# A decoder layer on one core: where the rotary products of q and k are made

## What is computed

```python
x = x + attention(layernorm(x))            # 16 heads of 32, rotary, causal
x = x + ssm(ctx, gate=layernorm(x))        # 16 states for each of 512 channels, gated
x = x + ffn(layernorm(x))                  # ternary weights, absmax scaling, exact gelu
```

```python
q, k, v = layernorm(x) @ w_qkv
rotary(x) = concat(x1 * cos - x2 * sin, x2 * cos + x1 * sin)
scores = rotary(q) @ rotary(k).T / sqrt(32)      # causal, softmax, @ v, @ w_o
```

## Time and profile before

| | |
|---|---|
| median of 3 runs | 1167.27 us (1163.96 to 1167.78) |
| the profiled execution | 1165.5 us |
| its span | 1163.7 us |
| busy in the span | TensorE 987.3 us, VectorE 956.9, ScalarE 808.1, GpSimd 623.8 |
| granted TensorE clock, mean | 0.921 |

### The profile page before, as it was taken

How to read it: one execution, slowest core, us unless ns; L and a number is a source line. 1 busy time by engine, 2 the same in 40 slices (tenths; PEclk the granted TensorE clock), 3 DMA queues, 4 the chain that set the end, 5 groups by cost and what they waited for, 6 DMA issues and landing times.

```text
span 1163.7 us, 18250 instructions
## 1 busy us (share of the span) xinstructions
PE 987.3 (85%) x5652; PEld 737.4 (63%) x5652; DVE 956.9 (82%) x1351; ACT 808.1 (69%) x1539; POOL 623.8 (54%) x509
## 2 busy tenths in 40 slices
PE   6857988789988999788999877586698889889997
PEld 3335765557755677655568656464577777778875
DVE  6458699884689976897997899899999999999654
ACT  5534787765488666798776998746988878884432
POOL 1257367764336667546665762476655555554411
PEclk8878989899989999889999986688898999899999
DMA  6215552444325653333464361430111110000000
GB/s 204 95 37 168 186 163 84 132 129 155 106 84 167 198 164 109 101 106 121 129 197 157 95 220 50 154 119 14 49 49 36 32 34 22 33 19 10 19 19 19
DMA packets 59358, 115.87 MB, mean 100 GB/s; under 512 B 8880, under 2 KB 13232, under 8 KB 58240
## 3 DMA queue, kind: packets, MB, share of 16 engines
q1 hardware_dynamic: 59264, 114.70, 31.4%
HBM read 90.42 MB, written 24.25 MB: 99 GB/s over the span
## 4 chain that ended last, share of the span: by engine, by line
PE 48%; DVE 21%; issue 11%; POOL 9%; ACT 8%; DMA 1%; SPq 1%; DVEq 0%; POOLq 0%; ACTq 0%
PE ps L1642 9%; PE ps L1710 6%; DVE hb L1804 5%; PE ps L1723 5%; PE ps L1784 5%; PE ps L1656 4%; PE ps L1682 4%; DVE y_acc L1826 4%; POOL hb L1253 3%; PE ps L1695 3%; PE ps L1774 3%; PE ps L1764 2%; DVE m_col L1900 2%; DVE fh L2030 2%; PE ps L1668 2%
## 5 line engine op out<-in xcount | busy, mean ns | idle before, releaser
L1253 POOL TENSOR_TENSOR hb<-du,b_bc 128x1024 f32<-128x1024 f32 (+1 forms) x160 | 313.4, 1978 | 175.0 <-PE ps L1710 174.2
L1804 DVE TENSOR_TENSOR_SCAN hb<-ps,hb 128x1024 f32<-128x1024 f32 (+1 forms) x128 | 257.7, 2015 | 31.2 <-ACT ps L1382 21.8
L1382 ACT ACTIVATE ps<-delta,a_neg 128x511 f32<-128x511 f32 (+2 forms) x320 | 180.0, 598 | 76.3 <-DVE hb L1804 69.1
L1710 PE MATMUL ps<-ident,hb 128*128 128x128 f32 x1088 | 169.6, 299 | 49.1 <-DVE hb L1804 20.3
L1826 DVE SCALAR_TENSOR_TENSOR y_acc<-ps,ct,y_acc 128x512 f32<-128x512 f32 x256 | 182.6, 742 | 29.2 <-PE ps L1710 28.2
L1710 PEld LDWEIGHTS ps<-ident,hb 128*128 128x128 f32 x1088 | 135.2, 153 | 80.2 <-issue 42.2
L1493 ACT ACTIVATE p_q<-ps,m_col 128x512 f32<-128x512 f32 (+3 forms) x256 | 131.4, 526 | 27.7 <-DVE m_col L1900 24.9
L1642 PE MATMUL ps<-xn_t,w_ring 128*128 128x512 f32 x256 | 124.4, 632 | 3.7 <-DVE tmp L1881 1.8
L1682 PE MATMUL ps<-ident,p_q 128*128 128x128 f32 x640 | 97.6, 298 | 22.7 <-ACT p_q L1493 17.9
L1509 ACT ACTIVATE p_t<-ps 128x512 f32<-128x512 f32 x160 | 87.8, 597 | 40.2 <-PE ps L1682 39.6
L1774 PE MATMUL ps<-t_fc,xq_hi 128*128 128x512 f32 x256 | 106.4, 416 | 10.0 <-DVE xq_lo L2015 6.5
(11 more groups left out here) (147 smaller groups left out, 1953.2 us busy)
## 6 DMA issues: line engine op xcount, KB each, us to landing
w_ring<-in_w_attn SPq DMA_DIRECT2D x32, 512.0 KB, 3.8
qk_d<-hl SPq DMA_DIRECT2D x64, 256.0 KB
q_st<-qk_d SPq DMA_DIRECT2D x128, 128.0 KB, 2.7
b_bc<-bc_d SPq DMA_DIRECT2D x48, 256.0 KB, 3.5
k_st<-qk_d SPq DMA_DIRECT2D x64, 128.0 KB, 2.7
k_st<-qk_d SPq DMA_DIRECT2D x128, 64.0 KB, 2.3
x_in<-in_x SPq DMA_DIRECT2D x16, 256.0 KB, 3.1
raw_fc<-in_w_fc SPq DMA_DIRECT2D x4, 1024.0 KB, 7.9
```

What stands on the lines that cost most here:

```text
L1253: nc.gpsimd.tensor_tensor(piece_of(e, hi, lo).rearrange("p (a n) -> p a n", a=2), du[b % 2][:, 2 * h:2 * h + 2, lo:hi], b_bc[:, i % BC_RIN ...
L1382: ins = nc.scalar.activation(factors(j, hi, lo)[:, (hi - lo) * m + start:(hi - lo) * (m + 1)], delta[b % 2][:, et, lo + start:hi], ACT.Exp ...
L1710: mm = nc.tensor.transpose(bank(kind, *a)[:, P * et:P * et + P], piece_of(2 * r + et // 2, hi, lo)[:, at:at + P], ident[:])
L1804: v.tensor_tensor_scan(h, d, h, 0.0, ALU.mult, ALU.add).then_inc(scan_done, 1)
```

## The change

In batches two to four (b > 0) a ScalarE item `rot` takes each half out of PSUM with one copy, to `tmp[:, 2]` and `tmp[:, 3]`. When the second half has been copied, GpSimd multiplies both by cosine into `tmp[:, 0:2]`, then by sine in place, and goes on with the subtraction and the addition as before. Batch one stays with VectorE. The plan is told 0.6 us for each ScalarE copy and 7 us for GpSimd's step instead of 2.6, and the VectorE shares of 1.4 us are gone. The count of freed banks now asks `emptied_by(item)` for the engine.

```diff
@@ WEIGHT @@
- 'act': {'carry': -3.3,
+ 'act': {'rot': 0,
+         'carry': -3.3,
...
+def rot_by(b):
+    return "act" if b > 0 else "dve"
+
+def emptied_by(item):
+    return rot_by(item[1]) if item[0] == "rot" else EMPTIED_BY.get(item[0])
@@ follows @@
         yield "pe", 3.5, [act("ln1b", b, LT - 1), sp("wload", CHUNK_OF[kind, b, n])]
-        yield "dve", 1.4, [pe(*item)] + ([dve("rot", b, n, 0)] if half else [])
+        who = rot_by(b)
+        yield who, 1.4 if who == "dve" else 0.6, [pe(*item)] + ([(who, ("rot", b, n, 0))] if half else [])
         if half:
-            yield "pool", 2.6, [dve(*item)]
+            yield "pool", 2.6 if who == "dve" else 7, [(who, item)]
@@ plan @@
-        reader = READER.get(kind) or (kind == "ht" and y_reader(item))
+        reader = emptied_by(item) or READER.get(kind) or (kind == "ht" and y_reader(item))
...
-    for _n, _item in enumerate(x for x in ORDER[_who] if EMPTIED_BY.get(x[0]) == _who):
+    for _n, _item in enumerate(x for x in ORDER[_who] if emptied_by(x) == _who):
@@ gpsimd, kind == "rot" @@
                     emptied(pool, TASK[(kind, *a)])
+                    if rot_by(b) == "act":
+                        halves = tmp[:, 2:4, :]
+                        consts(pool, "rotary")
+                        nc.gpsimd.tensor_tensor(tmp[:, 0:2, :], halves, cos[:].unsqueeze(1).to_broadcast([P, 2, L]), ALU.mult)
+                        own.done(nc.gpsimd.tensor_tensor(halves, halves, sin[:].unsqueeze(1).to_broadcast([P, 2, L]), ALU.mult))
+                        own.settle()
                     nc.gpsimd.tensor_tensor(tmp[:, 0, :], tmp[:, 0, :], tmp[:, 3, :], ALU.subtract)
@@ scalar @@
+                elif kind == "rot":
+                    b, n, half = a
+                    if half == 0:
+                        scratch_free(act, (kind, b, n))
+                    act.wait_ge(m_full, TASK[(kind, *a)] + 1)
+                    nc.scalar.activation(tmp[:, 2 + half, :], bank(kind, *a), ACT.Copy).then_inc(m_free["act"], 1)
```

## The result

| | before | after |
|---|---|---|
| median of 4 runs | 1165.62 us (1162.73 to 1167.78) | 1196.64 us (1193.46 to 1199.44) |
| span of the profiled execution | 1163.7 us | 1194.6 us |
| granted TensorE clock, mean | 0.921 | 0.912 |

The change costs 31.0 us, a ratio of 1.0249 [1.0219, 1.0279]. The direction was forecast; the time lies above the range, and the forecast's +8 us is about a quarter of what came. Beside the first, third, fourth and fifth experiment two of before's thirteen executions were slow (2378 and 2986 us); they are in no ratio, and without them before's median there is 1165.74 us and not 1166.18.

What follows compares the result with a forecast made beforehand. Rotary stretches were taken as bound by TensorE and VectorE in turn. Against 1165.5 us: -8.0 (products off the chain) + 6.6 (copies) + 9.5 (GpSimd, half) = +8.1, said as 1174 us; range 1157 to 1188, the forecast case's own 1170 to 1188.

Steps and rivals of the forecast that it cites:

- the pieces of VectorE's products on the chain: Rotary stretches: 19 pieces of VectorE's PSUM products, at 11 of 24 halves, come off the last-ending chain, -8.0 us.
- What is late next: Scratch tile between rotary pairs: held 4.0 us longer a pair, 16 us a batch; later loads costed at nothing.
- the lower end is nothing, for the order is worked out anew: GpSimd's longer rotary step: replanning can put ScalarE's hi copy behind other work, so the added cost could be nothing.
- half of 19.0 us taken for GpSimd: GpSimd's longer rotary step: middle of 0 and 19.0 taken as its cost, 9.5 us.
- a gain or loss of several us: Stretches without rotary pairs: the order worked out anew may gain or lose several us there.
- if the order stays: GpSimd's longer step at four of twelve pairs on the chain: 4 x 4.74 = 19.0 us, the upper end.
- 17.6 with the exchange: Rotary stretches: exchanging VectorE products for ScalarE copies, -1.4 us, with GpSimd's full 19.0 gives +17.6.
- VectorE's relief: Rival, rotary stretches: GpSimd's addition is absorbed and freed VectorE decides, 1150 to 1163 us; chance 0.30.
- the two cancel: Rival, rotary step: hidden on both sides, time within 0.3%, 1164 to 1171 us; chance 0.17.
- The scratch tile's chain: Rival, queues behind each batch's pairs: late by 16 us, 16 to 48 us lost, 1181 to 1213 us; chance 0.08.
- a sign of the forecast: Rotary stretches: more waits of VectorE's scans for GpSimd's product would show the forecast right.
- the Trainium skill's warning: VectorE and GpSimd share a port, so moving work might not help; by it alone +16 us.

Runs made afterwards that it cites:

- the first: Kernel before, only the plan told 7 us instead of 2.6 for GpSimd's rotary step in batches two to four: 1191.78 us, +25.6, 1.0202.
- third: Kernel before plus four extra GpSimd products of 128x512 behind each lo of batches two to four, outside the scratch tile, planned: 1191.82 us, +25.6, 1.0212.
- fourth: Kernel before, scratch tile in batches two to four passed on only when the pair's store has landed, plan told: 1207.08 us, +40.9, 1.0331.
- fifth experiment: Changed kernel, ScalarE's copies of the next pair wait only for GpSimd's rotary step, not for lo, plan told: 1166.64 us, +0.5, 1.0005.
- five new orders: Before's instructions replanned: GpSimd's step told as 2.9 us (+12.1) or 7 us (+25.6), or planner constant PATIENCE 0.28 (+26.4), 0.32 (+35.1), 0.34 (+13.2) instead of 0.3.
- the kept order: Changed kernel planned with before's engine and times, only the 24 halves moved from VectorE's list to ScalarE's at their planned times: 1209.30 us, +41.1, 1.0351.
- in four: After's instructions planned with planner constant PATIENCE 0.28 (+31.4), 0.3 (+31.0, the change itself), 0.32 (+29.2) and 0.34 (+27.3), against before.
- the early release: Next pair's ScalarE copies wait only for GpSimd's rotary step, not lo: after replanned +0.5 (PATIENCE 0.3), +0.4 (0.32); after in before's order 1210.25 us, +42.0.
- ten orders with the late release: Before's instructions in five new orders and after's in five, scratch tile freed at lo: 12 to 51 us above before.
- the four with 0.32 and 0.34: Planner constant PATIENCE 0.32 and 0.34 instead of 0.3: before's instructions +35.1 and +13.2, after's +29.2 and +27.3, against before.
- The early release with 0.32: Changed kernel with copies waiting only for GpSimd's rotary step, planner constant PATIENCE 0.32 instead of 0.3: 1168.51 us, +0.4, 1.0001 against before.
- before's order at 0.3: The unchanged kernel before, planned with planner constant PATIENCE at its original 0.3: 1165.62 us.
- before with early release: Kernel before, scratch rows exchanged between pairs so the next pair's first half waits only for GpSimd's step, plan told: 1165.64 us, -0.9, 0.9987.

## Why the forecast was right in sign and too small

**Right: the operations.** All four GpSimd durations and the copies were right, and the busy totals of GpSimd and ScalarE within 3 us. The step's four products are gone from VectorE's rows (32.8 us), but its busy time fell by 20.4 and not 33. A part of the gap of 12.4 is an overlap of the records that I did not allow for. Before, timeline of VectorE, two products of one half, 0.61 us apart though each lasts 0.69:

```profile
562.68 0.69 DVE L1880 TENSOR_TENSOR tmp<-ps,cos 128x512 f32<-128x512 f32 x1 [0.78 <-PE ps L1642]
563.29 0.68 DVE L1881 TENSOR_TENSOR tmp<-ps,sin 128x512 f32<-128x512 f32 x1
```

At 0.08 us for each of 48 that is at most 3.8 us. The last section has another 5.6; some 3 us stay open. Much of this is the order's: before's own instructions have a busy VectorE of 957.1 to 966.1 us in their five new orders, and in the kept order the change's fell by 27.3 (956.9 to 929.6). One reading of the rows was off without effect: the pieces of VectorE's products on the chain are 21, not 19; their 8.0 us and the 11 halves are right.

**Failed step: "What is late next", put into the sum at nothing.** The prediction had seen that the tile is held 4.0 us longer a pair, 16 us a batch, and that eight of nine passages are tight; it gave the hold no term of its own, costed the late loads behind the pairs at nothing "while TensorE has scan transposes to run", and left the rest to a rival with 0.08. It is what the loss goes with: the pairs of a batch spread by 6.7, 7.5 and 8.9 us, the fourth `lo` is late by 12, 19 and 31, and with the tile released early the same instructions are at +0.5 and +0.4. The way was another than told there. The projection does not start when the tile is free, but where the plan has put it, which is at the planned release; no engine of after waits for the tile.

**Failed step: "the lower end is nothing, for the order is worked out anew", and half of 19.0 us taken for GpSimd.** The new order was counted as free cover. It does cover: `hi` waits 14.3 us in after and 48.5 in the kept order, and the time is 10 us less. But it has a price of its own, which the sum lacked. Before's own instructions lose 12 to 35 us in five new orders (+12.1, +13.2, +25.6, +26.4, +35.1, mean 22.5), and after's, in four, 27 to 31 (mean 29.7). A fifth order of after's instructions, with 2.6 us told, lost 51.2; it is left out of that mean because its told time is far from the real one, though the 7 us told to before's (+25.6) is in the other. The last paragraph of the prediction allowed for "a gain or loss of several us" from this; on before's own instructions it is larger than any term of the sum, and I gave it no line there. What is left for the change itself is 29.7 - 22.5 = 7 us, or 4.4 by the paired values, near the forecast's 8.1 (up to the first `fc`: 25.7 - 18.5 = 7.2). With before's orders spread over 23 us, no run shows that this agreement is more than luck; with the fifth order counted it would be 34.0 - 22.5 = 11.5.

**Failed step: the upper end "if the order stays", 19.0 us (17.6 with the exchange).** It measured 41.1. I charged the 4.74 us to the four pairs at which before's chain runs through GpSimd. But that chain shows who was last then, and a longer step is last elsewhere too. GpSimd's result comes 4.0 us later at each of twelve pairs (4.74 less the 0.77 of the shorter ScalarE copy), and `hi` waits 43.8 / 12 = 3.65 us longer: by that the queues held some 0.3 us in hand on average. 12 x 4.0 = 48 us, less that, would have been the bound to write down. That these waits are what makes the 41.1 is argued and not shown; the 25.1 us at the copies stand beside them.

**The rivals.** VectorE's relief did not decide, nor did the two cancel. The scratch tile's chain, given 0.08 and 1181 to 1213 us, is the one that fits: 1196.6 lies in its range, and a shorter hold told to the plan, with the long step kept, takes all of the loss back in two orders. It is not shown that the hold does this by itself. With the order kept, the early release changed nothing (+42.0 for +41.1), and no run has the order of the early release with the late wait. Nor does all that an unfitted order loses come from this tile: ten orders with the late release lie 12 to 51 us above before, but the four with 0.32 and 0.34 lose 9 to 10 us of it behind the last pair. The early release with 0.32 loses 7.6 there too, behind 4.8 us gained ahead of the first `fc`. What I had against this rival, TensorE idle for a tenth only, was no argument: TensorE does other work while the pairs slip, and pays behind them, with 11.5 us more of idle time between the last pair and the first `fc`, which starts at 828 us and not at 796.

**Also not as forecast.** The scans did not wait more for GpSimd's product (4.3 us between 187 and 640 us before, 4.2 after). They did with the early release, 19.3 us, in the kernel that loses nothing: the wait named as a sign of the forecast is no sign of the loss. In after they waited for ScalarE's exponentials, and VectorE's accumulation for TensorE's transposes; before, then after:

```profile
DVE y_acc L1826 <- PE ps L1710: 16.2, 18, 4.0
...
DVE hb L1804 <- ACT ps L1382: 12.7, 12, 2.5
```

```profile
DVE y_acc L1851 <- PE ps L1735: 39.0, 33, 4.4
DVE hb L1829 <- ACT ps L1400: 29.6, 19, 4.9
```

ScalarE's own new wait is in front of the copy, 27.9 us for TensorE's projection, which I had not named. Before, it was VectorE that waited for the same projections (20.9 us at the first half's products); now exponentials are queued behind the wait. Of the Trainium skill's warning about moving work from VectorE to GpSimd (Perfetto Trace Analysis, Optimizing Scalar/DVE Operations), the advice fits after and not the early release. Its reason, the shared port, was not what decided: the early release has the same operations on the same engines and loses nothing.

**Open.** How the 31.0 us divide between new order and longer step, and whether the early release would still give them back in an order not planned for it. And why before's order at 0.3 is free of the loss at the late release: no single stretch of it shows that. No kernel here beats before clearly; the nearest is before with early release, 0.9987 [0.9970, 1.0005].

## What to carry to other kernels

Where every engine runs an order fixed in advance, price a longer step at each place where another engine's queue has its consumer at the head, in all its instances, not only where the old chain shows it. An order that is unusually good for its kernel is lost with small changes to the inputs of the planner; here all five tried cost 12 to 35 us. So judge a change by several orders of both versions, or with the order kept. Before a step in a shared buffer is made longer, release the parts of the buffer that its readers are done with; with the order planned anew for it that was worth 29 to 31 us here, the whole loss; in a kept order it was worth nothing.

## What the runs showed of the hardware

Operations of VectorE from SBUF to SBUF are held up beside GpSimd by more than the 1.4 us of the earlier trace rows. After, timeline around 730 us:

```profile
728.89 5.66 POOL L1265 TENSOR_TENSOR hb<-du,b_bc 128x1024 f32<-128x1024 f32 x2 [7.66 <-PE ps L1735]
729.61 2.73 DVE L1993 TENSOR_SCALAR low<-raw_fc,nthr 128x2048 bf16<-128x2048 f32 x1
732.37 4.33 DVE L1995 SCALAR_TENSOR_TENSOR t_fc<-raw_fc,thr,low 128x2048 fp32r<-128x2048 f32 x1
```

The two VectorE operations had means of 1.28 and 2.35 us before, and the pair of GpSimd's takes 4.68 in the earlier trace rows: all are longer where they meet. Groups by shape, before and then after:

```profile
L1842 DVE TENSOR_SCALAR x_in<-x_in,mv,rstd 128x512 f32<-128x512 f32 x16 | 12.2, 762 | 1.8 <-POOL rstd L1302 1.8
...
L1970 DVE SCALAR_TENSOR_TENSOR t_fc<-raw_fc,thr,low 128x2048 fp32r<-128x2048 f32 x4 | 9.4, 2351 | 0.1
...
L1968 DVE TENSOR_SCALAR low<-raw_fc,nthr 128x2048 bf16<-128x2048 f32 x4 | 5.1, 1282 | 0.0
```

```profile
L1867 DVE TENSOR_SCALAR x_in<-x_in,mv,rstd 128x512 f32<-128x512 f32 x16 | 13.4, 843 | 1.3 <-POOL rstd L1320 1.3
L1995 DVE SCALAR_TENSOR_TENSOR t_fc<-raw_fc,thr,low 128x2048 fp32r<-128x2048 f32 x4 | 11.4, 2845 | 0.1
...
L1993 DVE TENSOR_SCALAR low<-raw_fc,nthr 128x2048 bf16<-128x2048 f32 x4 | 7.5, 1880 | 0.0
```

Together that is 5.6 us of VectorE's missing relief. The products out of PSUM that batch one kept show nothing of the kind (0.68 to 0.69 us each). The Trainium skill (SBUF — State Buffer, Who interferes with whom) says that a VectorE operation with two SBUF inputs contends with a GpSimd operation that reads SBUF, that one in a mode with two ports contends with GpSimd, and that whichever issues first keeps the shared ports while the other is blocked. By that rule either side of such a meeting can get longer, and the products with one input in PSUM do not. The trace agrees: 5.66 us for 4.68 on one side, 2.73 and 4.33 for 1.28 and 2.35 on the other, and 0.68 to 0.69 for the products.
